# Reciprocals spread by a reduction, attention shares added in TensorE's accumulation, and two pieces of work at other places in the order

## The chip, the cores and the metric

The kernel runs on one core of a Trainium2 chip. The metric is the device time of one execution in microseconds; the kernel before took 362.46 us, the median of three executions (359.36, 362.46 and 364.48). A core has a matrix engine (TensorE, PE in the rows; PEld is its weight load), VectorE (DVE), ScalarE (ACT), GpSimd (POOL) and SyncE (SP), which here only issues transfers. Each engine takes its own instructions in the order in which they are written and waits for others by semaphores.

## The reference

One decoder layer on `x` of 4 batches, 256 tokens, 256 features, with a layer norm behind each of three parts:

```python
x = _layernorm(x + attn(x))          # 16 heads of 16
x = _layernorm(x + xattn(x, ctx))    # context of 64 tokens
x = _layernorm(x + moe(x))           # 64 experts, 8 per token
```

The first attention adds two shares, a linear one (the "memory") and a softmax one:

```python
mem_out = einsum('bhsd,bhde->bhse', q_feat, memory) / denom
attn = einsum('bhqk,bhkd->bhqd', softmax(scores), v)
g = sigmoid(gate)
combined = g * mem_out + (1.0 - g) * attn
return combined.reshape(B, S, H) @ Wo.T
```

The context attention is a masked softmax over 64 context tokens, projected by `wo` and gated by `sigmoid(rmsnorm(x) @ wg.T)`. The last part sends each token to 8 of 64 experts, at most 64 tokens per expert, and adds the weighted results.

## The kernel before

Nothing schedules the work: each engine's block is written by hand, and `pipelined` calls its `iteration(a, b, c)` for overlapping batches: batch `c` is projected and rotated, batch `a` runs its self-attention, and batch `b = a - 1` its context attention and routing. The calls are (-, -, 0), (0, -, 1), (1, 0, 2), (2, 1, 3), (3, 2, -), and then `last_batch(3)` does the context attention of batch 3 in halves of 128 tokens. Behind 243 us the 32 pairs of experts follow. `need(engine, name, batch, k)` is a wait until semaphore `name` has its `k`-th count of that batch (all of them without `k`), `prev` a wait for the batch before.

A batch's tokens lie as 128 partitions by 2 tiles (`NT`), its features as 2 tiles (`NC`). Of PSUM, `SA` and `SB` hold the scores by turns and, in their halves, the turned shares and the output projection; `O` holds projections and the memory's result, `M` all of the context attention.

What the change touches, in the order of a stage:

- The first scores go through `SA` and `SB` by turns, and VectorE takes their maxima (`score_max`, L984). The maxima are split in two bf16 parts (L1159, L1161), turned by TensorE (`maxima_turned`), and copied into the last rows of `q_op`, half by ScalarE (L761) and half by VectorE (L1166). The second scores (`second`) wait for both (`nmax_rows`, `nmax_rows2`).
- The context weights: VectorE subtracts the maxima (L975, L977), ScalarE takes the exponentials (L694), TensorE turns them (L1595) and ScalarE moves them (L698). VectorE sums them (L1044), takes the reciprocals (L1048) and spreads those from one per head to 16 equal columns per head, `rsum_w` (L1050). TensorE turns `rsum_w` (L1613), ScalarE moves it (L703), and L1057 scales the context result with it.
- `memory_out` on VectorE: three instructions (L1033, L1035, L1038) scale the memory share `mix_a` by gate and denominator. ScalarE fills `mix_a` and `r_lin` at the very start of the stage.
- `mix` on VectorE: L1138, L1140, L1143 scale the softmax share into `mix_b`, and L1146 adds both into `mixed`. TensorE turns `mixed` (L1441 into `SB`, four transposes), ScalarE moves it (L809), and TensorE projects it with `w_sb["o"]` on top of the residual.
- `context_keys` on POOL (L526, twice): it spreads the next batch's context keys by head into `xk_blk`; it waits for the last context scores of the present batch. POOL also computes the low bf16 parts of the next batch's queries and keys (L589, L595), issues the indirect DMAs of the routed rows of batch `b - 1` into `xin_d` (L535), and works out the norms' scales (L505 to L520).
- `spare_products` are products on TensorE whose results nobody reads.

The SBUF area `middle` is later overwritten by expert weights; `carve` gives out pieces of it one behind another.

## Time and profile before

| | |
|---|---|
| median of three executions | 362.46 us (359.36 to 364.48) |
| profiled execution: span of the core | 357.4 us |
| profiled execution: its own time | not given apart from the span; the median is 5.1 us above the span |
| mean granted TensorE clock | 0.921 |
| TensorE busy | 266.9 us (75%), 1869 instructions |
| VectorE busy | 225.8 us (63%), 516 |
| ScalarE busy | 142.9 us (40%), 258 |
| POOL busy | 167.5 us (47%), 179 |
| stages | set-up and batch 0 to 69 us; then about 47, 47 and 43 us for batches 1 to 3; last context attention 206 to 243; experts 243 to 336; final norm to the end |

### The profile page before, as it was taken

To read this page: it belongs to the slowest core of one execution; us is meant where nothing else is said; L and a number is where in the kernel's file an instruction comes from. 1 tells how busy PE (TensorE), PEld (TensorE's weight loads), DVE (VectorE), ACT (ScalarE), POOL (GpSimd) and SP (SyncE) were. 2 spreads that over 40 slices of the span, in tenths; PEclk is the share of its full clock that TensorE was granted. 3 is DMA by queue.
4 is the path that set the end of the run, shared out by engine and by line. 5 is a ranking of instruction groups with operands and counts; after the bars stand their busy time and mean duration, and the time that the engine had idled before them with its cause. 6 is when DMAs were issued, how large, how long until landed. Compare 5 with 4: busy or idle time off the path is not lost.

```text
span 357.4 us, 5633 instructions
## 1 busy us (share of the span) xinstructions
PE 266.9 (75%) x1869; PEld 166.6 (47%) x1869; DVE 225.8 (63%) x516; ACT 142.9 (40%) x258; POOL 167.5 (47%) x179
## 2 busy tenths in 40 slices
PE   7566695999889998889959777567999999960000
PEld 4353463767557766476636455223355454520000
DVE  0926756189966699766991767701367777730792
ACT  4600275226954259642386335101134444440022
POOL 2021022220252664836546276777535688883272
PEclk9995899899999999999999999898999999995555
DMA  7899907789999222777714399172599997666981
GB/s 234 253 123 263 341 21 120 107 274 328 388 312 167 97 92 75 146 113 257 277 68 133 92 307 316 52 208 56 155 299 312 180 152 123 73 72 122 367 318 59
DMA packets 47262, 66.62 MB, mean 186 GB/s; under 512 B 5979, under 2 KB 33241, under 8 KB 47234
## 3 DMA queue, kind: packets, MB, share of 16 engines
q1 hardware_dynamic: 39120, 56.52, 56.4%
q0 software_dynamic: 7680, 9.47, 14.1%
q8 instruction: 15, 0.25, 0.3%
q10 hardware_dynamic: 434, 0.27, 0.3%
q14 instruction: 13, 0.11, 0.1%
HBM read 36.45 MB, written 28.75 MB: 182 GB/s over the span
## 4 chain that ended last, share of the span: by engine, by line
PE 46%; DVE 23%; issue 9%; ACT 9%; DMA 8%; SPq 3%; POOL 1%; POOLq 0%; DVEq 0%; ACTq 0%
PE M L1391 18%; PE O L1391 8%; PE SB L1391 6%; PE SA L1391 5%; DVE nmax L984 5%; PE O L1871 3%; DMA early<-early 2%; ACT probs L671 2%; SPq L390 2%; DVE early L1351 2%; DMA xin_d<-att_f,idx_last 2%; DMA early<-acc_d 1%; DVE xmax L975 1%; DMA early<-weights 1%; DMA acc_d<-xp_t,idx_out 1%
## 5 line engine op out<-in xcount | busy, mean ns | idle before, releaser
L535 POOL DMA_INDIRECT xin_d<-row,idx_slot x48 | 47.7, 993 | 29.9 <-issue 12.4
L630 POOL DMA_INDIRECT acc_d<-xp_t,idx_out x32 | 49.5, 1546 | 23.3 <-DVE idx_out L1319 10.6
L1391 PE MATMUL M<-ones_sq 128*128 128x512 bf16 x125 | 33.8, 408 | 1.4 <-POOL mhalf L485 1.4
L1391 PE MATMUL M<-middle 128*128 128x256 f32 (+3 forms) x144 | 27.1, 369 | 4.7 <-DMA middle<-router 1.4
L1391 PE MATMUL SA<-early 96*128 96x256 bf16 (+1 forms) x128 | 21.1, 291 | 9.6 <-DMA early<-early 5.2
L589 POOL TENSOR_TENSOR early<-early 128x1024 f32<-128x1024 f32 x3 | 6.4, 2140 | 44.7 <-ACT early L681 44.7
L869 ACT ACTIVATE xp<-M 128x96 f32<-128x96 f32 x32 | 8.0, 250 | 46.0 <-PE M L1391 46.0
L984 DVE TENSOR_REDUCE nmax<-SA 128x4 f32<-128x1024 f32 x16 | 19.5, 1219 | 10.6 <-PE SA L1391 10.6
L1391 PEld LDWEIGHTS M<-middle 128*128 128x128 f32 (+1 forms) x144 | 19.4, 189 | 11.9 <-issue 5.9
L984 DVE TENSOR_REDUCE nmax<-SB 128x4 f32<-128x1024 f32 x16 | 19.5, 1220 | 4.9 <-PE SB L1391 4.9
L1391 PE MATMUL SB<-early 96*128 96x256 bf16 (+1 forms) x128 | 20.6, 286 | 1.5 <-ACT probs L671 0.6
L1391 PE MATMUL O<-middle,early 128*128 128x256 f32 (+1 forms) x96 | 20.7, 361 | 1.2 <-DVE middle L1024 0.6
L1391 PEld LDWEIGHTS SA<-early 96*128 96x128 bf16 (+1 forms) x128 | 11.3, 101 | 19.2 <-DMA early<-early 5.6
L1391 PEld LDWEIGHTS M<-ones_sq 128*128 128x128 bf16 x125 | 12.5, 105 | 15.5 <-issue 5.8
L1324 DVE COPY xp_t<-O 128x256 f32<-128x256 f32 x32 | 13.6, 425 | 8.0 <-PE O L1871 7.2
L1391 PEld LDWEIGHTS O<-middle,early 128*128 128x128 f32 x96 | 16.3, 197 | 4.5 <-DVE middle L1024 1.6
L548 POOL DMA_INDIRECT xin_d<-att_f,idx_last x16 | 15.6, 972 | 4.9 <-issue 4.3
L1328 DVE SCALAR_TENSOR_TENSOR xp<-xp,M 128x96 f32<-128x96 f32 x32 | 8.1, 254 | 14.5 <-ACT xp L869 14.5
L1351 DVE TENSOR_TENSOR early<-early 128x768 f32<-128x768 f32 x8 | 7.6, 955 | 14.8 <-DMA early<-acc_d 14.7
L761 ACT ACTIVATE early<-SB 32x1024 bf16<-32x1024 bf16 x8 | 7.7, 1004 | 21.5 <-PE SB L1491 21.5
L899 ACT ACTIVATE early<-early 128x256 f32<-128x256 f32 x8 | 4.8, 600 | 28.1 <-DVE early L1370 28.1
L1391 PEld LDWEIGHTS SB<-early 96*128 96x128 bf16 (+1 forms) x128 | 12.1, 101 | 7.8 <-issue 2.0
(269 smaller groups left out, 622.1 us busy)
## 6 DMA issues: line engine op xcount, KB each, us to landing
acc_d<-zeros SPq DMA_DIRECT2D x3, 2176.0 KB, 17.0
early<-early SPq DMA_DIRECT2D x48, 128.0 KB, 4.9
early<-acc_d SPq DMA_DIRECT2D x24, 256.0 KB, 6.0
xin_d<-zeros SPq DMA_DIRECT2D x1, 5136.0 KB, 19.0
early<-wgu SPq DMA_DIRECT2D x12, 384.0 KB, 6.7
middle<-wgu SPq DMA_DIRECT2D x12, 384.0 KB, 5.4
probs<-xin_d SPq DMA_DIRECT2D x20, 160.5 KB, 3.6
gu_sb<-wgu SPq DMA_DIRECT2D x8, 384.0 KB, 6.4
```

The costliest lines, as they stand in the source:

```text
L390: sp.dma_start(op[n * HD:(n + 1) * HD].rearrange("d (h c) t -> d h (c t)", h=HC), parts[:, w, part].rearrange("p c t -> p (c t)")).then_in ...
L535: nc.gpsimd.indirect_dma_start(xin_d, bass.IndirectOffsetOnAxis(ap=idx[:, t, k:k + 1], axis=0), rows[:, t, :], None, bounds_check=SLOTS - ...
L548: nc.gpsimd.indirect_dma_start(xin_d, bass.IndirectOffsetOnAxis(ap=idx_last[:, t, k:k + 1], axis=0), row_last[:, t, :], None, bounds_check ...
L630: nc.gpsimd.indirect_dma_start(acc_d[p % CHAINS], bass.IndirectOffsetOnAxis(ap=idx_out[:, p:p + 1], axis=0), yw[:, p % YRING, :], None, bo ...
L761: nc.scalar.activation(q_op[SPLIT_ROWS:P, 4 * i:4 * i + 4], SB[0:32, 0:512].bitcast(BF16)[:, 0:T].unsqueeze(1).broadcast_to([32, 4, T]), A ...
L869: nc.scalar.activation(htanh[:, p % 2, :], M[:, p % 2, 0:INNER], ACT.Tanh, scale=0.5).then_inc(S["htanh"], 1)
L984: nc.vector.tensor_reduce(nmax[:, 2 * g:2 * g + 2, :].rearrange("p h t -> p (h t)"), slot[g % 2][:].rearrange("p (n k) -> p n k", k=T), AX ...
L1324: nc.vector.tensor_copy(xin[:, p % 2].rearrange("p c s -> p (c s)"), O[:, p % 2, 0:D]).then_inc(S["xin"], 1)
L1328: nc.vector.scalar_tensor_tensor(hgate[:, p % 2, :], htanh[:, p % 2, :], 1.0, M[:, p % 2, 0:INNER], ALU.add, ALU.mult).then_inc(S["hgate"], 1)
L1351: nc.vector.tensor_tensor(fin[:, t, 0:3], fin[:, t, 0:3], fin[:, t, 3:6], ALU.add).then_inc(S["fpair"], 1)
L1391: return nc.tensor.matmul(o, l, r, start=start, stop=stop)
L1871: m = nc.tensor.transpose(O[:, p % 2, c * P:(c + 1) * P], gath(p)[:, c * P:(c + 1) * P], ident)
```

## The change

Four things change, and nothing else:

1. `rsum_w` (for the batches before the last) is written by a `tensor_reduce` with addition over an axis of length one, instead of a `tensor_scalar` that multiplies by 1.0.
2. The addition L1146 and the tile `mixed` are gone. TensorE adds instead: `share_turned` clears 512 columns of `SB` by a product with zeros and then adds the products of `mix_a` with the identity; later it adds those of `mix_b` on top. A product of a share (as the held operand) with the identity is that share, turned. The first part stands behind the attention's turn, the second at the place of the old turn. `mixed_f` and `xf` move by 512 words in `middle`; what is behind them keeps its place.
3. `memory_out` is written behind the split of the maxima, ahead of the wait for the turned maxima.
4. `context_keys(b + 1)` on POOL is written behind the slot DMAs that wait for the first scores, ahead of those that wait for the second.

```diff
--- before.py
+++ after.py
@@ -112,9 +112,10 @@
         rsum_f = carve([NC, T], of="middle")
         assert taken["middle"] == MID * GU_W
         mix_b = carve([NT, NH, HD], of="middle")
-        mixed = carve([NT, D], of="middle")
         mixed_f = carve([NC, T], of="middle")
         xf = carve([NC, T], of="middle")
+        assert taken["middle"] <= MID * GU_W + LATE_GRP * WD_W
+        taken["middle"] = MID * GU_W + LATE_GRP * WD_W
         router_sb = carve([NC, E], of="middle")
         con = sb("con", [P, CONST_W])
         identb = sb("identb", [P, P], BF16)
@@ -283,7 +284,7 @@
             xf_in=16, xt_in=16, qk_mm=1, v_mm=1, rot=2, rope=2, v_ev=1, high=1, rest_r=1, mid=1, low=1,
             op_in=16 * 2 * SPLIT_ROWS // HD, fmin=1, fexp=1, feat=1, kfeat_mm=1, kfeat_ev=1,
             mem_mm=1, memory=1, lin_mm=1, s1_mm=GRP, s1_max=GRP, nmax_hi=1, nmax_lo=1, nmax_mm=1, nmax_rows=2, nmax_rows2=2,
-            s2_mm=GRP, s2_exp=GRP, av_mm=GRP // 2, att_ev=2, att_mm=1, r_lin=4, r_att=2, mix=2, mixed=1, mixed_mm=1, mixed_ev=1, o_mm=1,
+            s2_mm=GRP, s2_exp=GRP, av_mm=GRP // 2, att_ev=2, att_mm=1, r_lin=4, r_att=2, mix=2, mixed_mm=1, mixed_ev=1, o_mm=1,
             res1=1, stats=4, mv=4, var=4, rstd=2, shift=4, x1=2, x1_mm=1, x1_ev=1,
             xq_mm=1, xq_ev=1, gate_mm=1, gate_th=2, kblk=2, x_mm=2, xmax=2, xsub=2, xexp=2,
             xpt_mm=2, xpt_ev=2, xav_mm=2, rsum=NT + 2, rsum_mm=1, rsum_ev=1, xatt=1, xo_mm=1, ygate=1, res2=1,
@@ -572,6 +573,8 @@
                             into_slots(b - 1, idx_slot, row, (0,), (n, n + 1))
                         need(pool, "s1_max", a)
                         into_slots(b - 1, idx_slot, row, (1,), (0, 1))
+                    context_keys(b + 1)
+                    if b >= 1:
                         need(pool, "s2_exp", a, 2)
                         into_slots(b - 1, idx_slot, row, (1,), (2, 3))
                         need(pool, "s2_exp", a, 4)
@@ -594,7 +597,6 @@
                     need(pool, "mid", c)
                     nc.gpsimd.tensor_tensor(parts[:, :, 2], rest[:], parts[:, :, 1], ALU.subtract).then_inc(S["low"], 1)
                 if b is not None:
-                    context_keys(b + 1)
                     norm_scale(b, 2)
 
             def norm_scale_of(b, t):
@@ -1047,8 +1049,9 @@
                         need(dve, "rsum", b, NT)
                         nc.vector.reciprocal(rsum[:], rsum[:]).then_inc(S["rsum"], 1)
                         need(dve, "rsum", b, NT + 1)
-                        nc.vector.tensor_scalar(rsum_w[:], rsum[:].unsqueeze(3).broadcast_to([P, NT, NH, HD]), 1.0, None, ALU.mult
-                                                ).then_inc(S["rsum"], 1)
+                        nc.vector.tensor_reduce(rsum_w[:].rearrange("p t h d -> p (t h) d"),
+                                                rsum[:].rearrange("p t h -> p (t h)").unsqueeze(2).unsqueeze(3).broadcast_to([P, NT * NH, HD, 1]),
+                                                AX.X, ALU.add).then_inc(S["rsum"], 1)
 
                 def context_out():
 
@@ -1142,10 +1145,6 @@
                     need(dve, "r_att", a)
                     nc.vector.tensor_tensor(mix_b[:], att[:, :, :, 0:HD], r_att[:].unsqueeze(3).broadcast_to([P, NT, NH, HD]),
                                             ALU.mult).then_inc(S["mix"], 1)
-                    need(dve, "mix", a)
-                    nc.vector.tensor_tensor(mixed[:].rearrange("p t d -> p (t d)"), mix_a[:].rearrange("p t h d -> p (t h d)"),
-                                            mix_b[:].rearrange("p t h d -> p (t h d)"), ALU.add).then_inc(S["mixed"], 1)
-
                 if a is not None:
                     for g in range(7):
                         score_max(g)
@@ -1160,6 +1159,7 @@
                     need(dve, "nmax_hi", a)
                     nc.vector.tensor_tensor(nmax_parts[:, :, 1, :], by_t, nmax_parts[:, :, 0, :], ALU.subtract
                                             ).then_inc(S["nmax_lo"], 1)
+                    memory_out()
 
                     need(dve, "nmax_mm", a)
                     for i in range(2, 4):
@@ -1184,8 +1184,6 @@
                         low_part()
                 if a is not None and b is None:
                     centred()
-                if a is not None:
-                    memory_out()
                 if b is not None:
                     context_out()
                     second_norm()
@@ -1523,6 +1521,16 @@
                                    probs_of(2 * q + r // 2)[:, r % 2, k, :], k == 0, k == NT - 1)
                     m.then_inc(S["av_mm"], 1)
 
+                def share_turned(share, first_of_two):
+
+                    if first_of_two:
+                        mm(SB[:, 0:512], ones_sq[:], zeros[:, 0:D].bitcast(BF16), True, False)
+                    for t in range(NT):
+                        for n in range(NC):
+                            i = mm(SB[:, n * T + t * P:n * T + (t + 1) * P], share[:, t, n * HC:(n + 1) * HC].rearrange("p h d -> p (h d)"),
+                                   ident, False, not first_of_two and t == NT - 1 and n == NC - 1)
+                    return i
+
                 def attention_turned(half):
                     need(pe, "att_ev", a, half + 1)
                     if half == 0:
@@ -1723,6 +1731,11 @@
                     attention_turned(0)
                     weighted(3)
                     attention_turned(1).then_inc(S["att_mm"], 1)
+                    need(pe, "s2_exp", a)
+                    need(pe, "mix", a, 1)
+                    if b is None:
+                        pe.wait_ge(S["zeroed"], 1)
+                    share_turned(mix_a, True)
                 if b is not None:
                     router_rows()
                 if c is not None and a is None:
@@ -1733,8 +1746,8 @@
                 if b is not None:
                     router_scores()
                 if a is not None:
-                    need(pe, "mixed", a)
-                    turn(SB[:, 0:512], mixed).then_inc(S["mixed_mm"], 1)
+                    need(pe, "mix", a)
+                    share_turned(mix_b, False).then_inc(S["mixed_mm"], 1)
                     if c is not None:
                         values()
                     need(pe, "xt_in", a)
```

VectorE in the stage of batch 1, around the maxima (`early` is the area with `q_op`, `rot_a`, `qk`; `middle` under L1050 is `rsum_w`). Before:

```order
L984 TENSOR_REDUCE nmax<-SB 128x4 [waits s1_mm]
L1159 CAST nmax_parts<-nmax 128x2x16 [waits nmax_lo,s1_max]
L1161 TENSOR_TENSOR nmax_parts<-nmax,nmax_parts 128x2x16 [waits nmax_hi]
L1166 COPY early<-SB 32x1024 [waits nmax_mm]
L1166 COPY early<-SB 32x1024
L975 TENSOR_REDUCE xmax<-M 128x16 [waits x_mm]
L977 TENSOR_TENSOR xp<-M,xmax 128x1024 [waits xmax]
L1044 TENSOR_REDUCE rsum<-xp 128x2x2x4 [waits xexp]
```

and the lines that follow the rotation, before:

```order
L1048 RECIPROCAL rsum<-rsum 128x32 [waits rsum]
L1050 TENSOR_SCALAR middle<-rsum 128x512 [waits rsum]
L1016 SCALAR_TENSOR_TENSOR early<-early 128x1024 [waits lin_mm,fexp]
L1033 RECIPROCAL r_lin<-r_lin 128x32 [waits r_lin]
L1035 TENSOR_TENSOR r_lin<-r_lin,gate_mem 128x32 [waits r_lin]
L1038 TENSOR_TENSOR mix_a<-mix_a,r_lin 128x512 [waits r_lin]
L1057 TENSOR_TENSOR middle<-M,middle 128x512 [waits rsum_ev,xav_mm]
```

The same place around the maxima, now (lines are two further on or less):

```order
L986 TENSOR_REDUCE nmax<-SB 128x4 [waits s1_mm]
L1158 CAST nmax_parts<-nmax 128x2x16 [waits nmax_lo,s1_max]
L1160 TENSOR_TENSOR nmax_parts<-nmax,nmax_parts 128x2x16 [waits nmax_hi]
L1035 RECIPROCAL r_lin<-r_lin 128x32 [waits r_lin]
L1037 TENSOR_TENSOR r_lin<-r_lin,gate_mem 128x32 [waits r_lin]
L1040 TENSOR_TENSOR mix_a<-mix_a,r_lin 128x512 [waits r_lin]
L1166 COPY early<-SB 32x1024 [waits nmax_mm]
L1166 COPY early<-SB 32x1024
L977 TENSOR_REDUCE xmax<-M 128x16 [waits x_mm]
L979 TENSOR_TENSOR xp<-M,xmax 128x1024 [waits xmax]
```

The three instructions on `r_lin` and `mix_a` moved from between L1016 and L1057 to between the split of the maxima and the wait for `nmax_mm`.

TensorE at the end of the same stage, before:

```order
L1532 MATMUL SA<-con,att_f 128x128 [waits att_ev]
L1532 MATMUL SA<-con,att_f 128x128 x3
L1441 MATMUL M<-con,middle 128x128 [waits res2]
L1441 MATMUL M<-con,middle 128x128 x3
L1560 MATMUL O<-con,early 128x128 [waits att_ev,feat]
L1560 MATMUL O<-con,early 128x128 x3
L1391 MATMUL M<-middle 128x64 [waits x2_ev]
L1391 MATMUL M<-middle 128x64 x3
L1441 MATMUL SB<-con,middle 128x128 [waits mixed]
L1441 MATMUL SB<-con,middle 128x128 x3
L1391 MATMUL O<-early,middle 128x256 x4
```

and now:

```order
L1540 MATMUL SA<-con,att_f 128x128 [waits att_ev]
L1540 MATMUL SA<-con,att_f 128x128 x3
L1389 MATMUL SB<-zeros,ones_sq 128x512 [waits mix,s2_exp]
L1389 MATMUL SB<-con,mix_a 128x128 x4
L1439 MATMUL M<-con,middle 128x128 [waits res2]
L1439 MATMUL M<-con,middle 128x128 x3
L1568 MATMUL O<-con,early 128x128 [waits att_ev,feat]
L1568 MATMUL O<-con,early 128x128 x3
L1389 MATMUL M<-middle 128x64 [waits x2_ev]
L1389 MATMUL M<-middle 128x64 x3
L1389 MATMUL SB<-con,middle 128x128 [waits mix]
L1389 MATMUL SB<-con,middle 128x128 x3
L1389 MATMUL O<-early,middle 128x256 x4
```

A product with zeros and four products of `mix_a` stand between the attention's turn and the turn of the second norm's rows; the four transposes of `mixed` have become four products of `mix_b`.

POOL in the stage of batch 1, before:

```order
L526 TENSOR_TENSOR middle<-middle,con 128x512 [waits x_mm,consts,xk_ev]
L526 TENSOR_TENSOR middle<-middle,con 128x512
L589 TENSOR_TENSOR early<-early 128x1024 [waits high]
L595 TENSOR_TENSOR early<-early 128x2x512 [waits mid]
L526 TENSOR_TENSOR middle<-middle,con 128x512 [waits x_mm]
L526 TENSOR_TENSOR middle<-middle,con 128x512
L509 TENSOR_SCALAR nrm<-mv 128x2 [waits x1,mv]
```

and now:

```order
L527 TENSOR_TENSOR middle<-middle,con 128x512 [waits x_mm,consts,xk_ev]
L527 TENSOR_TENSOR middle<-middle,con 128x512
L527 TENSOR_TENSOR middle<-middle,con 128x512 [waits x_mm]
L527 TENSOR_TENSOR middle<-middle,con 128x512
L592 TENSOR_TENSOR early<-early 128x1024 [waits high]
L598 TENSOR_TENSOR early<-early 128x2x512 [waits mid]
L510 TENSOR_SCALAR nrm<-mv 128x2 [waits x1,mv]
```

The two pairs of `xk_blk` instructions, for the present and the next batch, stand one behind the other; in the stages of batches 2 and 3 five pairs of slot DMAs are ahead of them.

## Rows read from the trace of the kernel before

**Rows 1.** The page, chain that ended last: shares of the span by engine.
```profile
PE 46%; DVE 23%; issue 9%; ACT 9%; DMA 8%; SPq 3%; POOL 1%; POOLq 0%; DVEq 0%; ACTq 0%
```

**Rows 2.** Timeline, tail of batch 0: start, us, engine, line, op, out<-in, count [idle before].
```profile
57.35 2.52 POOL L595 TENSOR_TENSOR early<-early 128x1024 bf16<-128x1024 f32 x1 [3.88 <-ACT early L685]
...
60.68 0.69 DVE L1146 TENSOR_TENSOR middle<-mix_a,middle 128x512 f32<-128x512 f32 x1
...
61.43 0.65 PE L1441 MATMUL SB<-con,middle 128*128 128x128 f32 x4 [2.16 <-DVE middle L1146]
...
61.92 3.34 PE L1391 MATMUL O<-early,middle 128*128 128x256 f32 x8
```

**Rows 3.** Timeline, tail of batch 1.
```profile
108.37 0.66 PE L1441 MATMUL SB<-con,middle 128*128 128x128 f32 x4
...
108.87 1.89 PE L1391 MATMUL O<-early,middle 128*128 128x256 f32 x8
...
114.40 2.10 PE L1391 MATMUL M<-ones_sq 128*128 128x512 bf16 x9
```

**Rows 4.** Windows, TensorE: stretch, length, busy (instructions), granted clock, DMA share, GB/s.
```profile
62.00:66.00 4.00, 4.00 (x11) 0.57 1.15 133
```

**Rows 5.** Timeline, reciprocals spread and what follows, batch 1.
```profile
95.62 2.14 POOL L589 TENSOR_TENSOR early<-early 128x1024 f32<-128x1024 f32 x1 [21.35 <-ACT early L681]
...
95.96 2.08 DVE L1050 TENSOR_SCALAR middle<-rsum 128x512 f32<-128x512 f32 x1
...
99.57 0.63 ACT L703 ACTIVATE middle<-M 128x512 f32<-128x512 f32 x1
...
100.70 0.68 DVE L1057 TENSOR_TENSOR middle<-M,middle 128x512 f32<-128x512 f32 x1
```

**Rows 6.** Timeline, the same in batch 2, and POOL beside the residual.
```profile
142.66 3.03 DVE L1050 TENSOR_SCALAR middle<-rsum 128x512 f32<-128x512 f32 x1
...
146.44 0.60 ACT L703 ACTIVATE middle<-M 128x512 f32<-128x512 f32 x1
...
146.74 0.34 DVE L1033 RECIPROCAL r_lin<-r_lin 128x32 f32<-128x32 f32 x1
...
147.95 0.68 DVE L1057 TENSOR_TENSOR middle<-M,middle 128x512 f32<-128x512 f32 x1
...
151.06 2.49 POOL L526 TENSOR_TENSOR middle<-middle,con 128x512 f32<-128x512 f32 x2
...
151.44 1.21 DVE L1067 SCALAR_TENSOR_TENSOR middle<-middle 128x512 f32<-128x512 f32 x1
```

**Rows 7.** Timeline, maxima and second scores, batch 1.
```profile
83.67 1.13 PE L1391 MATMUL M<-middle 64*128 64x256 f32 x8
...
84.39 0.19 DVE L1161 TENSOR_TENSOR nmax_parts<-nmax,nmax_parts 128x32 bf16<-128x32 f32 x1
...
85.17 1.28 DVE L1166 COPY early<-SB 32x1024 bf16<-32x1024 bf16 x2 [0.59 <-PE SB L1491]
...
87.33 0.60 PE L1391 MATMUL SB<-early 128*128 128x256 bf16 x4
...
87.74 1.22 DVE L977 TENSOR_TENSOR xp<-M,xmax 128x1024 f32<-128x1024 f32 x1
...
89.35 1.15 ACT L694 ACTIVATE xp<-xp,nrm 128x1024 f32<-128x1024 f32 x1
```

**Rows 8.** Timeline, context weights, batch 3.
```profile
181.90 1.22 DVE L977 TENSOR_TENSOR xp<-M,xmax 128x1024 f32<-128x1024 f32 x1
...
183.16 1.15 ACT L694 ACTIVATE xp<-xp,nrm 128x1024 f32<-128x1024 f32 x1
```

**Rows 9.** Source line L1140: count, ns min/median/max, first and last start, forms.
```profile
L1140 DVE TENSOR_TENSOR r_att<-r_att,gate_att x4: 191/192/661, 59.3 to 199.0; 128x32 f32<-128x32 f32 x4
```

**Rows 10.** Timeline, start of the last batch's context attention.
```profile
207.34 1.13 PE L1391 MATMUL M<-middle 128*128 128x128 f32 x8 [0.35 <-ACT middle L822]
...
208.45 1.08 POOL L535 DMA_INDIRECT xin_d<-row,idx_slot  x1 [0.18 <-issue]
```

## The prediction

> **What bounds the kernel now.** I read the chain of waits first, then the timeline of the four stages (stage n: batch n's attention, beside the context attention of batch n-1), tails before middles, then the granted clock. Below, "batch n" stands for its stage. The chain's shares by engine [rows 1] name TensorE with 46% and VectorE with 23%, and no queue: the four batches up to 206 us are a relay between these two and ScalarE, in which a microsecond counts only on the leg that is last at that moment. So each part of the change is priced per batch, at four legs: the maxima (VectorE), the context weights (VectorE, ScalarE), the tail (TensorE) and what POOL does beside them.
>
> In batch 0's tail the reader is to see TensorE stand still for 2.16 us until VectorE has scaled and added both attention shares, and then run the values' products in 3.34 us [rows 2]; the same products take 1.89 us in batch 1 [rows 3]. The clock column says why: 0.57 on average between 62 and 66 us [rows 4], so most of that stretch ran at 1.2 GHz and not 2.4. In batch 1's tail TensorE waits for nothing before the turn of the sum at 108.37 [rows 3]: there it is the bound.
>
> In the middle of batches 1 and 2 the spreading of the reciprocals (L1050) takes 2.08 and 3.03 us [rows 5, 6] for 512 elements. In batch 1 it ends 0.28 us behind POOL's L589 (95.62 + 2.14), which began before it [rows 5]. It waits for POOL.
>
> **The instruction that spreads the reciprocals.** Three uses. As a reduction over one element it should take what a pass over 512 elements takes elsewhere: 0.69 us (L1057, L1067 undisturbed, half of a 1.23 us pass over 1024 [rows 5 to 7]). No row shows a reduction with 512 outputs; below it are 0.5 us, above it nothing near, so I keep 0.7 and leave the upper end to a rival. What it gives back is small, since L1057 behind it needs ScalarE's L703 too. Batch 1: L703 ends at 100.20, L1057 started at 100.70. Batch 2: 147.04 against 147.95 [rows 5, 6]. So at most 0.5 and 0.9 us come back, and that is only because the memory scaling no longer stands between them.
> No row has a SBUF-to-SBUF reduction beside a POOL operation. The Trainium skill, "SBUF — State Buffer", section "Who interferes with whom", says that a reduction never takes the ports that VectorE and POOL share; by it the price is the same 0.7 us.
>
> **The memory scaling, moved up.** Its three instructions run from 146.74 to L1057's start, 1.2 us, 1.3 with the last one's tail [rows 6]. Now they start behind L1161, which ends at 84.58, where VectorE stood still until 85.17 for the turned maxima [rows 7]. So 0.6 of 1.3 us is hidden and 0.7 pushes the two L1166 copies to end at 87.2. TensorE's second scores for them start at 87.33: just in time. Behind them L977 ends at 89.7 instead of 88.96, and ScalarE's L694, at 89.35, starts 0.35 us late [rows 7]. ScalarE is without a gap from there to L703, so its 0.35 comes off the gains above: batch 1 gains 0.1, batch 2 0.5. In batch 3 L694 followed L977 within 0.04 us (183.12, 183.16 [rows 8]) and no later gain exists (no wait of L1050): it loses 0.7.
>
> **The context keys, moved up.** POOL's two operations, 1.0 us each (2.49 for two with a wait of 0.5 in them [rows 6]), wait only for the context scores. In batches 2 and 3 they come behind slot DMAs, late enough to meet nothing that waits. In batch 1 no slot DMAs exist: they start when TensorE ends the scores, 83.67 + 1.13 = 84.80, plus some 0.1 to wake [rows 7]. The scaling's second instruction, with two inputs in SBUF, starts 0.4 us behind 84.58, at 84.98. Rows show what two such neighbours do: the same kind of instruction, L1140, took 0.66 us at 59.3 where its median is 0.19 [rows 9], and ended as POOL's L595 did, at 59.9 [rows 2]; L1067 took 1.21 us inside POOL's two L526, where L1057, of its size, takes 0.69 [rows 6]: they take turns. So the small multiplication waits until 85.95, POOL's second operation goes next until 87.1, then the large one runs to 87.8, the copies to 89.15, and the second scores start 1.8 us late. I charge batch 1 with 1.8; bounds are 0 (no collision) and 2.4 (all of VectorE's delay, 2.6, reaches ScalarE less its slack).
> In exchange L1067 in batch 2 loses its 0.5 us wait, but TensorE is behind it in any case: nothing.
>
> **The sum inside TensorE's accumulation.** Removed: VectorE's L1146, 0.7 us, and a turn of 4 transposes, 0.50 us from start to start (108.37 to 108.87 [rows 3]). Added on TensorE: one product with zeros over 512 columns, 0.23 (2.10 / 9 [rows 3]), and twice 4 float products of 128 columns, which the trace counts as 8: 1.13 us with the tail [rows 10], 0.96 without it (the 4 transposes show 0.66 with it and 0.50 without). The first group stands at the end of the attention's turn, ahead of the second norm's rows, and costs 1.2; the second replaces the turn and adds 0.5. Together 1.65 us per batch on TensorE. In batches 1 to 3 nothing covers it: TensorE is the leg that ends last there, and the rows, the router and the state of the output all stand behind.
> The Trainium skill, "TensorE: Matmul & The Clock Gate", section "Terms", calls a transpose in its own mode four times faster than a float product; by that each group would be 2.0 us (4 x 0.50). The row of the same shape, 8 in 1.13 us, says otherwise, and I go by it; the rule has its rival below.
> In batch 0 the 2.16 us gap covers the first group. The scaling's third instruction no longer disturbs L595 (2.52 us here [rows 2], 2.14 for L589, of its size [rows 5]), so L1140 ends 0.4 earlier; the last share is ready at 60.3, the values start at 61.3 instead of 61.92: 0.6 us. And with 1.2 us more products before them, I expect the clock to stay up: the values at 1.89 instead of 3.34 us, and 0.25 on the products behind them, 1.7 together. The same page, section "Part 4: PE-mode transpose", says that transposes do not count as activity for the clock; before the fall TensorE had run mostly those, which agrees.
>
> **Sum**, against the profiled span of 357.4 us: batch 0: -0.6 - 1.7 = -2.3. Batch 1: +1.65 - 0.1 + 1.8 = +3.3. Batch 2: +1.65 - 0.5 = +1.1. Batch 3: +1.65 + 0.7 = +2.3. Total +4.4, a span of 361.8. After 206 us nothing is edited, and POOL's queue of slot DMAs, from 208.45 on [rows 10], starts with batch 3's output, so the 4.4 us arrive at the end. The span lies 5.1 below the median of 362.46; on that scale: **366.9 us**. The three runs shown spread from 359.36 to 364.48, and a comparison here can tell about 2%, 7.2 us, from no change.
>
> **Rivals.**
> 1. As summed, 0.46: 366.9.
> 2. No collision in batch 1, 0.20: VectorE and POOL are only 0.1 us apart there. 366.9 - 1.8 = 365.1.
> 3. The clock is not kept, or a like fall comes elsewhere, 0.14: the 2.16 us gap speaks for my case, the chance timing of the falls against it. 366.9 + 1.7 = 368.6.
> 4. TensorE has more air than I see, 0.12: the extra products fall into waits for ScalarE's copies (none is seen at 108.37). Three batches at 1.65 come back: 362.0, and 360.2 without the collision.
> 5. The reduction is slow per output, 0.05: it must end before TensorE's turn of the sums, some 1.5 us after it starts in batches 1 and 2. Up to there it costs nothing; beyond, each microsecond is two. At 3 us (6 ns per output) it adds 3: 369.9, above the 2% line at 369.7. Against it: L1050 itself had 2 and 3 us and lost little.
> 6. A float product of 128 columns costs four transposes, 0.03: 1.04 more per group, two groups, four batches, less 1 in batch 0's gap: 366.9 + 7.3 = 374.2. The row of 8 in 1.13 us speaks against it; it is the rule named above.
>
> Faster by over 2% (under 355.2) needs gains that no row offers: 0.02. Slower by over 2%: rivals 5 and 6 and the tails of 1 and 3: 0.12. Within 2%: 0.86. The range reaches from between rival 4's two values, 361.0, to beyond rival 3 and the foot of rival 5, 370.0; it leaves out rival 6 and the ends of 4 and 5.
>
> **What would show it.** Right: L1052 at 0.7 us in all three uses; the granted clock at 1.00 through 61 to 66 us and the values in about 1.9 us; the two groups of products on SB at about 1.13 us each, with the rows of the second norm 1.2 us further behind the attention's turn than before; in batch 1 one of the scaling's multiplications at 1 us or more beside POOL's context keys. Wrong: if the first group lies in a wait in batches 1 to 3, if batch 1's scaling takes 1.3 us in all, or if stretches behind 206 us change length, where nothing was edited.

## The result, and the profile after

The changed kernel takes **367.68 us** (median; executions 365.36 to 368.23), the kernel before 363.47 in the same comparison: ratio 1.0158, 95% interval 1.0116 to 1.0201. It is slower, by 1.2 to 2.0%. A second comparison, on another chip, gave 382.87 against 378.73 us, ratio 1.0120 (1.0048 to 1.0191). The medians differ by 4.2 and 4.1 us, against 4.4 forecast, and 366.9 was forecast for the time; taken by the ratios the differences are 5.7 us (4.2 to 7.3) and 4.5 us (1.8 to 7.2). Ratios count only executions within 1.5% of their kernel's fastest: this leaves out, among others, single ones of 443, 666 and 677 us, and the profiled ones of the reduction alone and of the version without zeros, of which only the legs are read. All ratios below are within one chip, since the chips differ: the kernel before took 381.0, 378.7 and 362.0 us beside the three sets of experiments.

The profiled execution took 367.51 us with a span of 365.5, 8.1 above the span before: twice the difference of the medians. So the trace has to be read leg by leg. The page's chain by engine, after:

```profile
PE 44%; DVE 21%; issue 10%; DMA 9%; ACT 9%; SPq 5%; POOL 1%; POOLq 0%; DVEq 0%; ACTq 0%
```

It answers to [rows 1]; it names no new bound. I use two marks in each batch that every kernel has: the last of the first scores' maxima on VectorE (L984, after: L986), and the move of the turned sum on ScalarE (L809, after: L811). Between two marks most legs repeat to 0.1 us from execution to execution and from chip to chip, which a time of the whole kernel does not; exceptions are named where they come. All in us, after less before:

| leg | before | after | difference | forecast |
|---|---|---|---|---|
| start to batch 0's last maxima | 39.94 | 41.62 | +1.68 | 0 |
| from there to the last share (L1143, after: L1146) | 20.02 | 21.00 | +0.98 | -2.3 with the next |
| from there to batch 1's last maxima | 22.96 | 21.50 | -1.46 | |
| batch 1, last maxima to move | 26.15 | 28.27 | +2.12 | +3.3 |
| batch 2 | 26.91 | 27.62 | +0.71 | +1.1 |
| batch 3 | 24.33 | 26.92 | +2.59 | +2.3 |
| behind it, to the end of the span | | | +1.5 | 0 |

Between a batch's move and the next one's last maxima lie 20.55 or 20.56 us in both, batches 1 and 2.

**Batch 0's tail**, after, TensorE's timeline (start, duration, what; the bracket is idle time and its releaser), against [rows 2]:

```profile
61.24 0.66 PE L1540 MATMUL SA<-con,att_f 128*128 128x128 f32 x4 [0.72 <-ACT att_f L691]
61.73 0.38 PE L1389 MATMUL SB<-zeros,ones_sq 128*128 128x512 bf16 x1
61.95 1.05 PE L1389 MATMUL SB<-con,mix_a 128*128 128x128 f32 x8
62.84 0.60 PE L1568 MATMUL O<-con,early 128*128 128x128 f32 x4
63.37 1.16 PE L1389 MATMUL SB<-con,middle 128*128 128x128 f32 x8
64.36 1.89 PE L1389 MATMUL O<-early,middle 128*128 128x256 f32 x8
```

The 2.16 us of standing still are gone, and the values take 1.89 instead of 3.34. The granted clock (last but two numbers of a row: clock, DMA share, GB/s) against [rows 4]:

```profile
62.00:66.00 4.00, 4.00 (x29) 3.65 (x28) 1.25 (x3) 1.19 (x2) 0.54 (x1) 1.00 0.92 144
```

Behind this tail batch 1's first scores now wait for the transfer of their operands; in the kernel before they start at 70.69 without a wait:

```profile
71.89 0.61 PE L1389 MATMUL SA<-early 96*128 96x256 bf16 x4 [0.28 <-DMA early<-early]
```

**Batch 1's maxima**, after, against [rows 7]:

```profile
84.12 1.21 DVE L986 TENSOR_REDUCE nmax<-SB 128x4 f32<-128x1024 f32 x1
86.07 0.19 DVE L1037 TENSOR_TENSOR r_lin<-r_lin,gate_mem 128x32 f32<-128x32 f32 x1
86.09 2.52 POOL L527 TENSOR_TENSOR middle<-middle,con 128x512 f32<-128x512 f32 x2 [11.07 <-PE M L1389]
86.30 1.42 DVE L1040 TENSOR_TENSOR mix_a<-mix_a,r_lin 128x512 f32<-128x512 f32 x1
87.75 1.28 DVE L1166 COPY early<-SB 32x1024 bf16<-32x1024 bf16 x2
```

The collision is there, smaller than forecast: the small multiplication began 0.02 us ahead of POOL and escaped (0.19); only the large one stood behind POOL's first operation, 1.42 us where it has 0.69 in the other three batches.

**Batch 1's tail**, after, against [rows 3]:

```profile
107.42 0.66 PE L1540 MATMUL SA<-con,att_f 128*128 128x128 f32 x4 [0.72 <-ACT att_f L691]
107.91 0.38 PE L1389 MATMUL SB<-zeros,ones_sq 128*128 128x512 bf16 x1
108.12 1.05 PE L1389 MATMUL SB<-con,mix_a 128*128 128x128 f32 x8
109.02 0.60 PE L1439 MATMUL M<-con,middle 128*128 128x128 f32 x4
111.25 1.11 PE L1389 MATMUL SB<-con,middle 128*128 128x128 f32 x8
112.39 0.60 ACT L811 ACTIVATE middle<-SB 128x512 f32<-128x512 f32 x1 [1.65 <-PE SB L1389]
```

The norm's rows (L1439) come 1.11 us behind the products with zeros, and no wait lies in front of them.

**The spreading**, all uses of the reduction (minimum, median, maximum in ns), against L1050 in [rows 5, 6]:

```profile
L1052 DVE TENSOR_REDUCE middle<-rsum x3: 686/686/686, 98.5 to 190.7; 128x512 f32<-128x512 f32 x3
```

**Behind batch 3.** All engines keep +6.62 us from the move of batch 3's share through the tail of that work, where nothing was edited, as forecast. The last 1.5 us come from the experts' scatters on POOL, of which some wait for an earlier one's transfer:

```profile
289.82 1.54 POOL L632 DMA_INDIRECT acc_d<-xp_t,idx_out  x1 [1.79 <-DMA acc_d<-xp_t,idx_out]
292.09 1.54 POOL L632 DMA_INDIRECT acc_d<-xp_t,idx_out  x1 [0.73 <-issue]
293.94 1.54 POOL L632 DMA_INDIRECT acc_d<-xp_t,idx_out  x1 [0.30 <-DMA acc_d<-xp_t,idx_out]
```

There TensorE, VectorE and ScalarE still stand at +6.3 while these stand at +8.5. I take that, the first two rows of the table and 0.4 us of batch 3 (the clock low from 188.4 to 191.8 us, no such stretch before) for chance. The experiments bear on each. From batch 3's move to the end of the span it takes 156.0 us in the kernel before and 157.5 in the changed one, but 155.8 in the kernel before again and 157.3 with the memory scaling alone or the sum in batch 0 alone, so the 1.5 us do not go with the change as a whole. The low clock in batch 3 is there in both second executions too (187.0 to 190.4 us in the kernel before).

### The profile page after: what moved, and what is told of

Same layout as the page of the kernel before. It is cut to its first block, busy times and chain, and to the rows that moved or that the text cites. A ratio compares the mean times of both kernels' runs of the same rounds, so it can differ in the third digit from the quotient of the medians.

```text
span 365.5 us, 5737 instructions
## 1 busy us (share of the span) xinstructions
PE 275.5 (75%) x1921; PEld 174.3 (48%) x1921; DVE 220.0 (60%) x512; ACT 143.3 (39%) x258; POOL 166.7 (46%) x179
## 4 chain that ended last, share of the span: by engine, by line
PE 44%; DVE 21%; issue 10%; DMA 9%; ACT 9%; SPq 5%; POOL 1%; POOLq 0%; DVEq 0%; ACTq 0%
PE M L1389 17%; PE SB L1389 7%; PE O L1389 7%; DVE nmax L986 6%; PE SA L1389 5%; SPq L391 4%; DMA early<-early 4%; PE O L1884 3%; DVE xmax L977 2%; DVE early L1349 2%; ACT probs L673 1%; DMA xin_d<-att_f,idx_last 1%; DVE early L1355 1%; DMA early<-acc_d 1%; DMA early<-weights 1%
## 5 line engine op out<-in xcount | busy, mean ns | idle before, releaser
L986 DVE TENSOR_REDUCE nmax<-SA 128x4 f32<-128x1024 f32 x16 | 19.5, 1218 | 11.1 <-PE SA L1389 11.1
L1389 PE MATMUL O<-middle,early 128*128 128x256 f32 (+1 forms) x96 | 22.5, 384 | 1.5 <-DMA early<-weights 0.8
L1389 PE MATMUL SB<-early 96*128 96x256 bf16 (+1 forms) x128 | 21.9, 300 | 1.9 <-DVE early L1166 0.9
L986 DVE TENSOR_REDUCE nmax<-SB 128x4 f32<-128x1024 f32 x16 | 19.5, 1218 | 6.3 <-PE SB L1389 6.3
L1389 PEld LDWEIGHTS O<-middle,early 128*128 128x128 f32 x96 | 17.5, 210 | 5.2 <-DVE middle L1026 1.6
```

The source lines that it names most:

```text
L986: nc.vector.tensor_reduce(nmax[:, 2 * g:2 * g + 2, :].rearrange("p h t -> p (h t)"), slot[g % 2][:].rearrange("p (n k) -> p n k", k=T), AX ...
L1389: return nc.tensor.matmul(o, l, r, start=start, stop=stop)
```

## The experiments

Theory: the sum of the rows as forecast. Chief rivals: TensorE had air, so that the products cost nothing in batches 1 to 3; and what looks like the change's work in batch 0 (clock, first maxima) is the chance of an execution. Where a single leg is quoted it is between the marks above.

**Sum back on VectorE** (the changed kernel with its part 2 undone; the edit is shortened):

```diff
+                    nc.vector.tensor_tensor(mixed..., mix_a..., mix_b..., ALU.add)
-                    share_turned(mix_a, True)
-                    share_turned(mix_b, False)
+                    turn(SB[:, 0:512], mixed)
```

> The changed kernel with the sum of the shares put back on VectorE (addition and turn as before); the reduction, the early memory scaling and the early context keys stay. Theory (TensorE ends the tails of batches 1 to 3, so its extra products are paid there): the tail of each of these batches, from the context result's scaling to the output's move on ScalarE, is 1.5 us shorter than in the changed kernel, 4.5 in all; batch 0's gap of about 2.2 us is back and costs 0.6, or 2.3 where the clock also falls. In all 2.2 to 3.9 us under the changed kernel, ratio to before 1.000 to 1.005. Rival (TensorE has air, the extra products lay in waits): tails of 1 to 3 keep their length, batch 0 loses 0.6 to 2.3, so 1 to 2 us above the changed kernel.

Measured: 379.4 us, ratio to before 0.9927 (0.9885 to 0.9968). Batch 1's leg is 26.80 instead of 28.27. From the last share to the move:

```profile
108.79 0.69 DVE L1147 TENSOR_TENSOR middle<-SA,r_att 128x512 f32<-128x512 f32 x1
110.28 0.66 PE L1444 MATMUL SB<-con,middle 128*128 128x128 f32 x4
110.97 0.60 ACT L812 ACTIVATE middle<-SB 128x512 f32<-128x512 f32 x1 [1.28 <-PE SB L1444]
```

2.18 us, where the changed kernel takes 3.66 from 108.73 to 112.39: **1.48 us** for the sum in TensorE. Air is refuted. Batch 2 shows 26.48 against 27.62, 1.14; 0.36 of the missing part is a later start of the context result's scaling, 0.46 instead of 0.10 us behind the ScalarE move that it needs, for which I know no cause. Batch 3 is not read, since the clock was low at its turn. In batch 0 a gap is back, and the clock did not fall:

```profile
64.38 0.66 PE L1444 MATMUL SB<-con,middle 128*128 128x128 f32 x4 [1.77 <-DVE middle L1150]
```

The gap is 1.77 us here and not 2.16. From the last share to batch 1's maxima it takes 21.27 us; the changed kernel takes 21.50. So in batch 0 too the sum in TensorE gained nothing over the sum on VectorE, once the other three parts were in.

**Context keys at the old place** (rest changed; in this edit and the next the comments stand for the places):

> The changed kernel with the context keys at their old place on POOL. Theory (POOL and VectorE take turns, and the keys' second operation held the large multiplication of the memory scaling in batch 1): that multiplication takes 0.69 instead of 1.42 us, the two copies of the maxima's rows start 0.7 us earlier, and 0.6 to 0.7 us of it reach the context result's scaling and the end of batch 1; batches 2 and 3 keep their length within 0.2. In all -0.6. Rival (given back): the keys at the old place hold the residual's instruction in batch 1's or 2's tail by 0.5 us and this reaches the end: 0.

```diff
-                    context_keys(b + 1)      # behind the first-score DMAs
+                    context_keys(b + 1)      # behind the low parts
```

Measured: 381.73 us, ratio 1.0037 (0.9992 to 1.0083). The legs are 27.54, 27.62 and 27.26 us. Batch 1's maxima:

```profile
85.89 0.19 DVE L1036 TENSOR_TENSOR r_lin<-r_lin,gate_mem 128x32 f32<-128x32 f32 x1
86.12 0.69 DVE L1039 TENSOR_TENSOR mix_a<-mix_a,r_lin 128x512 f32<-128x512 f32 x1
86.84 1.28 DVE L1165 COPY early<-SB 32x1024 bf16<-32x1024 bf16 x2
```

The collision costs 0.73 us at the copies and all of it, 0.73, at the end of batch 1. The ratio lies lower than the changed kernel's two by more than this explains. They were measured on other chips, and all four ratios of this set are lower than their legs would make them, so I rest on the legs.

**Memory scaling at the old place** (rest changed):

> The changed kernel with the memory scaling at its old place on VectorE. Theory (behind the split of the maxima it stands in front of the two copies that TensorE's second scores wait for): the copies start 0.7 us earlier in batches 0, 2 and 3 and 1.4 in batch 1; batches 0 and 3 become 0.7 shorter each, batch 1 gets 1.4 and gives 0.5 to 0.7 back ahead of the context result's scaling, batch 2 gets 0.7 and gives 0.9 back. In all -1.9 us. Rival (the place has no weight, since ScalarE's exponentials are the bound between): 0, and the copies' gain is gone at the last exponentials.

```diff
-                    memory_out()             # behind the split of the maxima
+                    memory_out()             # ahead of context_out()
```

Measured: 381.65 us, ratio 1.0016 (0.9980 to 1.0052). The copies come 0.75, 1.39, 0.72 and 0.72 us earlier, as expected; batch 1's leg is 27.64 (-0.63), batch 2's 27.85 (+0.23), batch 3's 26.74 (27.26 with the context keys late, on the same chip and with the clock at 1.00 in both legs). In batch 0 the last share stands 21.05 us behind the maxima, 21.00 in the changed kernel: the expected 0.7 there is not found. Batch 3's leg holds a late start on this chip, below, and is compared with that chip's alone.

**The reduction alone** (on the kernel before):

> The kernel before with the reduction alone. Theory: the reduction takes 0.69 us in all three uses and does not wait for POOL. In batch 1 nothing comes of it, because TensorE reaches the turn of the sums only 0.1 us before it does now; in batch 2 the turn comes 1.0 us earlier and 0.6 to 0.9 reach the context result's scaling; batch 3 loses 0.2 of slack that nothing waits for. In all -0.6 to -0.9, ratio 0.998. Rival A (the wait moves on): the residual or scaling instruction behind it waits for POOL as long as the spreading did, 0. Rival B (the reduction too waits for POOL): 2 and 3 us again.

Measured: 378.68 us, ratio 0.9925 (0.9883 to 0.9968). Batch 1's leg 26.16 (+0.01), batch 2's 26.79 (-0.12). In batch 2 the context result's scaling comes 0.33 us earlier, half of what was expected, and this is why:

```profile
147.55 0.69 DVE L1050 TENSOR_REDUCE middle<-rsum 128x512 f32<-128x512 f32 x1
148.12 2.17 POOL L589 TENSOR_TENSOR early<-early 128x1024 f32<-128x1024 f32 x1
149.94 1.44 DVE L1016 SCALAR_TENSOR_TENSOR early<-early 128x1024 f32<-128x1024 f32 x1 [1.71 <-ACT early L676]
150.46 1.79 POOL L535 DMA_INDIRECT xin_d<-row,idx_slot  x1 [0.17 <-issue]
```

The reduction takes 0.69 us beside POOL, here and in batch 1, where it lies wholly inside L589 (100.83 in 100.50 to 102.64); L1016 behind it, 1.21 before, now takes 1.44 and POOL's transfer issue 1.79 where the others take 0.97. Part of the wait moved on, as rival A had it. Rival B is out. The 0.1 us of these legs gives a ratio of 1.000; where the other 2.7 us of 0.9925 lie stays open.

**The changed kernel once more**, no edit:

> The changed kernel as it is, once more, as the measure for the kernels beside it and for which of its differences repeat. Theory (what the edits cause repeats to 0.1 us between the same two instructions, the clock's falls and the waits for transfers don't): from one move of the turned share on ScalarE to the next, batch 1 47.8, batch 2 48.2, batch 3 47.1 us plus what a fall of the clock adds; the large multiplication of batch 1's memory scaling takes 1.42 us again. Rival (the collision in batch 1 is a chance of 0.1 us): it takes 0.69 in this run. Ratio to before 1.01 to 1.02.

Measured: 382.87 us. Batches 1 and 2: 28.27 and 27.62 us, to the hundredth as before; the large multiplication 1.42 again; from the last share to batch 1's maxima 21.51 (21.50). The collision is no chance. Batch 3 took 28.25 instead of 26.92; a low clock lasted longer, and 0.65 us lie at one place:

```profile
199.12 0.60 ACT L705 ACTIVATE middle<-M 128x512 f32<-128x512 f32 x1
200.50 0.69 DVE L1060 TENSOR_TENSOR middle<-M,middle 128x512 f32<-128x512 f32 x1 [8.07 <-PE M L1389]
```

VectorE starts 0.78 us behind ScalarE's end; in the changed kernel's first trace 0.13 (L705 ends at 198.03, L1060 starts at 198.16). Nothing in the profile says for what it waits. All eight executions of this set and the one before start late there, by 0.78 to 0.95 us, and none of the six on the other two chips (0.13 or 0.14). Batch 3's legs are compared within a set for that reason.

**Five spare products in the kernel before's gap** (batch 0 only; the two waits are for the free `SB` and the zeros):

```diff
+                    if b is None:
+                        need(pe, "s2_exp", a)
+                        pe.wait_ge(S["zeroed"], 1)
+                        for _ in range(5):
+                            mm(SB[:, 0:512], ones_sq[:], zeros[:, 0:D].bitcast(BF16))
                     need(pe, "mixed", a)
                     turn(SB[:, 0:512], mixed)
```

> The kernel before with five products of zeros over 512 columns (0.22 us each, results unused) in batch 0's tail, ahead of the turn of the sum, where TensorE stood still for 2.16 us; nothing else. Theory (the fall of the clock behind the gap comes from TensorE standing still): the clock is 1.00 from 62 to 66 us, the values take 1.89 instead of 3.34 us, 1.7 us less in all, ratio 0.995. Rival (the fall hangs on something else, since the kernel with the sum on VectorE had the gap and no fall): the clock and the values are as they come, and the change has no part in them.

Measured: 378.03 us, ratio 0.9982 (0.9942 to 1.0022). TensorE:

```profile
62.97 1.24 PE L1391 MATMUL SB<-zeros,ones_sq 128*128 128x512 bf16 x5
65.29 0.66 PE L1441 MATMUL SB<-con,middle 128*128 128x128 f32 x4 [1.08 <-DVE middle L1146]
65.78 1.89 PE L1391 MATMUL O<-early,middle 128*128 128x256 f32 x8
```

From the last share to batch 1's maxima 21.26 us against 22.96 before: **1.70 less**, the term of the prediction; that it agrees to the hundredth is luck. The clock is 1.00 from 50.7 to 211 us. The whole kernel's interval holds both the expected 0.995 and 1. Batch 2's leg is 27.29 here against 26.91, where nothing was edited: the context result's scaling starts 0.6 us late, again without a cause that I know. Legs, too, have their chances.

**The first group where TensorE waits** (in the changed kernel, ahead of the attention's second turn):

```diff
                     weighted(3)
-                    attention_turned(1).then_inc(S["att_mm"], 1)
                     need(pe, "s2_exp", a)
                     need(pe, "mix", a, 1)
...
                     share_turned(mix_a, True)
+                    attention_turned(1).then_inc(S["att_mm"], 1)
```

> The changed kernel with the first group of share products (zeros and the memory share) ahead of the attention's second turn, where TensorE waits 0.72 us for ScalarE's move, instead of behind it. Theory (TensorE's time counts one for one in the tails of batches 1 to 3): 0.72 of the group's 1.2 us are hidden, the softmax share comes 0.47 later with no effect; each of the tails of batches 1 to 3 is 0.7 shorter than in the changed kernel, batch 0's up to 0.5 longer. In all -1.6 to -2.1. Rival (the later softmax share holds the second group): no gain, 0.

Measured: 380.2 us, 2.7 under the changed kernel on the same chip, ratio to before 1.0033 (0.9996 to 1.0071). The group ends as the turn starts, and nothing waits in front of the rows:

```profile
106.35 0.39 PE L1389 MATMUL SB<-zeros,ones_sq 128*128 128x512 bf16 x1
106.58 1.05 PE L1389 MATMUL SB<-con,mix_a 128*128 128x128 f32 x8
107.47 0.60 PE L1540 MATMUL SA<-con,att_f 128*128 128x128 f32 x4
107.91 0.60 PE L1439 MATMUL M<-con,middle 128*128 128x128 f32 x4
```

Legs 27.45, 26.79 and 27.43 (28.25 in the changed kernel beside it): 0.82, 0.83 and 0.82 less, where 0.7 was expected. TensorE's time counts one for one there. Over the three batches 2.5 us came back, where 2.1 was the most expected; the medians' 2.7 agree.

**And without the zeros** (`start` on the first product of the memory share alone):

> As the one before, and without the product of zeros: the first product of the memory share starts the accumulation. Theory: the group is 0.96 instead of 1.19 us; the turn is held by 0.25 instead of 0.47 us, and tails of batches 1 to 3 are 0.23 shorter each: 0.95 each under the changed kernel, batch 0 up to 0.3 longer. In all -2.6 to -2.9. Rival (the engine overlaps the zeros with the first loads of weights): the same as the one before.

Measured: 380.0 us, ratio 1.0013 (0.9966 to 1.0060). Legs 27.33 and 26.67 in batches 1 and 2: another 0.12 each, not 0.23. Batch 3's is 27.50, 0.07 longer than with zeros. The group now shows 1.16 us and runs from 106.80 to the turn at 107.80, 1.00, against 1.12 with zeros (106.35 to 107.47). So about half of the zeros' 0.23 us had cost nothing; with zeros the load of the share's weights is shown from 106.35 on, beside them. The whole kernel's time does not tell the two versions apart.

**The kernel before once more**, no edit:

> The kernel before as it is, once more. Theory (batch 0's gap of 2.16 us is there in every execution, and the clock falls behind it in some of them; the low stretches ahead of 42 us start when they start): the values of batch 0 take 1.9 us or over 3 us, batch 0's last maxima start between 41.2 and 41.8 us as in the six kernels run since, not at 39.94 as in the execution profiled first; from one move of the turned share to the next, batch 1 takes 45.25 us without a fall of the clock and about 47 with one, batch 2 47.5, batch 3 44.9. Rival (the changed kernel itself makes the first maxima late by 1.7 us): 39.9 again.

Measured: 361.84 us, ratio 0.9991 (0.9955 to 1.0027). Last maxima at 41.15 us, not 39.94 (the other kernels: 40.4 to 42.0): 1.2 of the changed kernel's +1.68 on that leg are there without any change, and nothing edited stands ahead of this mark, so I take the leg for chance. The +0.98 behind it goes with the clock. In the first trace that leg has the clock at 1.00 throughout, in the changed kernel's at 0.92 on average, and the context keys alone, with 0.92 too, take 20.95 us there (changed: 21.00). At 0.85 this kernel takes 22.46 and the changed one, run again, 22.22. Legs 26.14, 26.91 and 24.46. The fall came again, and lasted longer; from the last share to batch 1's maxima it takes 24.14 us, 2.9 more than with the spare products, so that a fall has no one price:

```profile
65.08 1.11 PE L1441 MATMUL SB<-con,middle 128*128 128x128 f32 x4 [2.16 <-DVE middle L1146]
65.99 3.62 PE L1391 MATMUL O<-early,middle 128*128 128x256 f32 x8
```

```profile
60.00:64.00 4.00, 2.16 (x24) 1.27 (x24) 2.88 (x8) 2.12 (x3) 2.52 (x1) 1.00 0.75 125
64.00:66.00 2.00, 0.92 (x5) 0.92 (x6) 0.99 (x2) 0.00 (x0) 0.00 (x0) 0.53 1.07 151
66.00:70.00 4.00, 4.00 (x10) 3.02 (x10) 0.00 (x0) 0.95 (x2) 0.00 (x0) 0.50 1.14 131
```

TensorE ran at 2.4 GHz, stood still for 2.16 us, and came back at 1.2. The fourteen profiled executions fall into groups by the place of the memory scaling. With the scaling late, the open gap of 2.16 us was followed by the fall in four of four (both of the kernel before, the reduction alone, the keys alone), the filled gap in none of three (memory scaling late, spare products, and batch 0 alone, next). With the scaling early, there was no fall with the gap filled (five executions), and none with it open either (two: sum back on VectorE, memory scaling alone). In these two the gap is only 1.77 us long, since the small multiplication of the softmax share, free of POOL, takes 0.27 us instead of 0.66. So in batch 0 the early scaling alone did as much for the clock as the filled gap.

**Batch 0 alone**, the version that the experiments point to (the kernel before, with the reduction, and `share_turned` only for batch 0; the edit is shortened, and VectorE keeps its addition for batches 1 to 3):

```diff
+                    if b is None:
+                        share_turned(mix_a, True)
...
+                    if b is None:
+                        share_turned(mix_b, False)
+                    else:
                         turn(SB[:, 0:512], mixed)
```

> The kernel before with the reduction, and with the sum in TensorE in batch 0 alone; batches 1 to 3 add on VectorE and turn as before, memory scaling and context keys stand at their old places. Theory: batch 0's tail 0.2 shorter and with the clock kept, 1.7 where the kernel before has the fall; batch 1 as before, batch 2 0.1 to 0.3 shorter, batch 3 as before: 0.3 to 2.2 us under the kernel before, 6 to 7 under the changed one up to the end of batch 3 on the same chip. Ratio to before 0.994 to 0.999. Rival (the sum in TensorE costs in batch 0 too): equal to before.

Measured: 361.45 us, ratio to before **0.9968 (0.9933 to 1.0002)**. From the last share to batch 1's maxima 21.04 us, legs 26.16, 26.78 and 24.98. Batches 1 and 2 and batch 0's tail show the gains and none of the costs; batch 3's leg is 0.5 to 0.6 us longer than in the kernel before, 0.45 of it at the turn of the sum, where the clock was low (from 201.9 us on). By the ratios to before (1.0120 and 1.0158 against 0.9968) it beats the changed kernel by 1.5 to 1.9%, across chips; from the kernel before it can't be told.

**The context keys alone** (on the kernel before):

> The kernel before with the context keys alone at their new place. Theory (they collide only with an early memory scaling): copies of the maxima's rows and the context result's scaling keep their times in batches 1 to 3 within 0.1 us; the residual's instruction in batch 2 takes 0.69 instead of 1.21 us and TensorE's rows do not come earlier by it; the norm's scale on POOL comes 0.4 us earlier in batch 1's tail and nothing waits for it: 0. Rival (the two operations hold the context maxima's subtraction or the copies, whoever is beside them): 0.7 in batch 1.

Measured: 361.77 us, ratio 0.9984 (0.9946 to 1.0023). Legs 26.16 and 24.31 in batches 1 and 3 (0.0); 26.68 in batch 2, 0.23 less. I had expected 0 there; the last share comes 0.19 earlier behind the freed residual instruction, and that reaches the move. There is no part of the collision without an early scaling.

**The memory scaling alone** (on the kernel before):

> The kernel before with the memory scaling alone at its new place. Theory (additive, from the kernels with one part undone): the copies are 0.7 us later in all four batches; no collision, the large multiplication takes 0.69 in batch 1; batch 0 gives all of it back, batch 1 -0.1, batch 2 -0.2, batch 3 +0.5 from the last maxima to the move of the turned share: +0.2 in all, ratio 1.000. Rival (the scaling takes the ports from POOL's or ScalarE's work behind the split and costs in every batch): +0.7 in each.

Measured: 362.18 us, ratio 1.0008 (0.9967 to 1.0049). Copies 0.76, 0.65, 0.72 and 0.72 us later; legs 26.34 (+0.19), 26.48 (-0.43) and 25.05 (**+0.72**). Batch 0's tail shows the short gap and no fall:

```profile
63.99 0.66 PE L1440 MATMUL SB<-con,middle 128*128 128x128 f32 x4 [1.77 <-DVE middle L1146]
64.48 1.89 PE L1390 MATMUL O<-early,middle 128*128 128x256 f32 x8
```

From the last share to batch 1's maxima it takes 21.31 us, 1.66 less than in the kernel before's first trace. Batch 3 keeps the whole delay (against the kernel before again, 24.46, it is 0.59):

```profile
180.02 0.69 DVE L1038 TENSOR_TENSOR mix_a<-mix_a,r_lin 128x512 f32<-128x512 f32 x1
180.74 1.28 DVE L1167 COPY early<-SB 32x1024 bf16<-32x1024 bf16 x2
...
184.58 1.15 ACT L694 ACTIVATE xp<-xp,nrm 128x1024 f32<-128x1024 f32 x1 [0.68 <-DVE xp L977]
```

ScalarE waits 0.68 us for L977, which it met within 0.04 in [rows 8].

## Why the prediction was right

The number came out (366.9 against 367.68, +4.4 against +4.2 and +4.1 for the difference), and most of it for the reasons given; one term was more than twice too large and smaller ones stood against it.

- **Products in the tails, +1.65 each.** Right in mechanism, 1.48 in size (undoing the sum), and shown to be TensorE's own time (moving the group into a wait gave 0.82 back per batch). The second group took 1.11 us, where [rows 10] had 1.13. The rule that a float product costs four transposes does not hold for these blocks: the changed kernel's 8 on `SB` took 1.11 us and the 4 transposes in their place 0.66 in the kernel with the sum on VectorE. Rivals 4 and 6 are out.
- **The collision, +1.8 in batch 1.** The step that failed in size: it cost **0.73**. It was priced from the order of arrival: POOL first, then by turns, both multiplications waiting. VectorE was first, by 0.02 us, and so had only one wait; and when POOL's first operation ended (87.16), VectorE's waiting multiplication went next, not POOL's second operation. The bounds 0 to 2.4 held it. It repeated in all five executions with both parts early (1.42 us each time, VectorE 0.02 ahead), presumably because both starts hang on the same chain.
- **Batch 0, -2.3.** The clock's part is 1.70, as forecast, and filling the gap alone gives it in the kernel before. The prediction gave it to the new products alone; in the changed kernel it is not theirs alone, since the early memory scaling, too, is enough: with the sum on VectorE and the scaling early the tail takes 21.27 and 21.31 us without a fall, and the changed kernel 21.50. The cover's part is 0.2 to 0.5 and not 0.6: from the last share to the move 1.94 us against 2.16, and up to the last share, at the same mean clock, 21.00 against 20.95 and 22.22 against 22.46. There the undisturbed small multiplication (0.27 us, 0.66 before) did give its 0.4, and the later copies, to which I had charged nothing, took most of it. Another 0.46 came back at once: batch 1's first scores now wait for the transfer of their operands (19.56 us from the move to the last maxima, 19.10 in kernels that don't wait). That wait stood in no rival. In all -1.5 to -1.7. That the fall belongs to the gap of 2.16 us rests on seven executions with the scaling late, four with the gap open and three with it filled. It did not follow the gap of 1.77 us, in two executions. The prediction set the fall beside the transposes that TensorE had run before it; the same transposes stood before the shorter gap, and no fall came, so the runs do not support them as the cause. What decides between 1.77 and 2.16 us, or whether more executions would show a fall behind the shorter gap, stays open.
- **Memory scaling.** Batch 3 +0.7: measured 0.72. The copies "just in time": late by 0.65 to 0.76. Together with the reduction, -0.1 in batch 1 and -0.5 in batch 2 were forecast. The parts alone give +0.19 and +0.01, and -0.43 and -0.12; in the changed kernel, where 1.48 for the sum and 0.73 for the collision are taken off, -0.09 and -0.77 are left.
- **The reduction.** 0.69 us three times, and in every other kernel that has it; it does not wait for POOL, rival 5 is out. That its gain is small was right, but not only because L1057 needs ScalarE: the instruction behind it took over a piece of the wait.
- **Context keys in batch 2, "nothing".** They gain 0.23 alone, and nothing beside the other parts (27.62 us with and without).
- **Nothing behind 206 us.** +6.62 at the move of batch 3's share and on through the work behind it, as forecast. But the scatters' stretch is 1.5 us longer, and a change of length there stood among the prediction's own signs of being wrong; kernels with single parts of the change differ there by as much among themselves, so I count it as chance.

By cause the traces give -1.46, +2.12, +0.71 and +2.21 (2.59 less the clock's 0.38), **+3.6 us**, of the span's +8.1; the other 4.5 are first maxima (1.68), the middle of batch 0 at a lower clock (0.98), batch 3's low stretch (0.38) and the scatters (1.5). The forecast's 4.4 is 0.8 above this sum: 1.2, 0.4 and 0.1 too much in batches 1, 2 and 3 (1.1 of it for the collision), and a gain in batch 0 that was 0.8 too large. That the forecast lies within 0.3 us of the medians' differences is in part luck: errors of 1.7 and 0.8 us cancelled, and single executions of one kernel spread over 3 to 6 us.

## What to carry to other kernels

Moving an addition from VectorE into TensorE's accumulation can pay only where TensorE stands still: here in the one batch with a gap, and in the other three it cost 1.5 us each. Even in that batch it gained only beside the late memory scaling; with the scaling early, the gap was shorter, the clock stayed up by itself, and the sum in TensorE cost 0.2. Two edits that each remove the same wait must not both be credited with it. Where TensorE does wait, put the new products in that wait; the same group of products, 1.1 us earlier in the order, was 0.8 cheaper. Price an edit between two marks of the trace, batch by batch: the legs of batches 1 and 2 repeated to 0.02 us in second executions of both kernels where the whole kernel's time scattered by 5, and two executions' spans differed by twice what the change did. One trace of a kernel is still not enough: two legs came out 0.4 us long without an edit that explains it.

## What the runs showed of the hardware that was not expected

- POOL's issue of an indirect transfer took longer beside VectorE's L1016 where L1016 had begun first: 1.79 us instead of 0.97 (reduction alone, begun 0.52 us behind L1016), 1.83 in the changed kernel (148.99, 0.26 behind). In the kernel before it began 0.05 us ahead of L1016 and took 0.99.
- The reduction over an axis of one takes 0.69 us for 512 elements where the multiplication by 1.0 took 0.50 at its shortest in the kernel before (batch 3: 185.99, beside a transfer issue of POOL's) and 0.43 with nothing of POOL's beside it (memory scaling alone: 187.40), and 2.08 and 3.03 beside POOL's L589 in the kernel before. It gives up 0.2 to 0.3 us and does not wait.
- Two chips were slower by 17 and 19 us for the same kernel (378.7 and 381.0 us against 362.0). In the changed kernel's two traces 16.3 us of it arise between 220 and 260 us, where ScalarE stands still for 3.4 us at a time; as releaser the profile has only "remote". Memory scaling late:

```profile
224.42 1.02 ACT L837 ACTIVATE xp_t<-O 128x1024 f32<-128x1024 f32 x1 [3.48 <-remote]
230.24 0.38 ACT L824 ACTIVATE middle<-M 128x256 f32<-128x256 f32 x1 [3.39 <-remote]
```
